# Pairwise dot products on TensorE: one product of four samples on 128 columns, or four products of one sample on 32 columns each

## The reference

```python
e = jnp.stack([tbl_0[ids[:, 0]], ..., tbl_31[ids[:, 31]]], axis=1)   # [2048, 32, 256]
dots = jnp.einsum('bnd,bmd->bnm', e, e)
z = dots[:, iu, ju]                        # i < j: 496 values for each sample
h = jnp.concatenate([z, dense_ctx], axis=1)                          # [2048, 512]
h = jnp.maximum(h @ W_top1 + b_top1, 0.0)                            # 512 -> 512
h = jnp.maximum(h @ W_top2 + b_top2, 0.0)                            # 512 -> 256
y = h @ W_top3                                                       # 256 -> 1
```

## Time and profile before

| | |
|---|---|
| median of 3 runs | 632.87 us (630.38 to 633.89) |
| profiled execution | 631.31 us, of it the span from the first to the last instruction 629.3 us |
| mean granted TensorE clock | 0.986 of full speed |
| busy: TensorE, weight loads | 558.0 us, 548.1 us |
| busy: GpSimd | 440.0 us |
| busy: VectorE, ScalarE | 358.6 us, 283.0 us |
| DMA | 70.29 MB, mean 112 GB/s |

### The profile page before, as it was taken

One profiled execution on the slowest core, in us unless ns is written; L12 is line 12 of the kernel. 1 busy time (PEld: TensorE's weight loads), 2 busy tenths in 40 slices (PEclk: granted clock), 3 DMA queues, 4 the chain that ended last, 5 costly groups with the idle time before them and its releaser, 6 DMA issues.

```text
span 629.3 us, 11634 instructions
## 1 busy us (share of the span) xinstructions
PE 558.0 (89%) x4752; PEld 548.1 (87%) x4752; DVE 358.6 (57%) x772; ACT 283.0 (45%) x497; POOL 440.0 (70%) x462
## 2 busy tenths in 40 slices
PE   0345989998999999999999999999999999998973
PEld 0335989898999999999999999999999999998973
DVE  0163846746476574838486675848385665735330
ACT  0171644543455454545454454546354454545330
POOL 6787777777777777777777777777777777777000
PEclk9999999998999999999999999999999999999987
DMA  8963443344444643446334543446334643355000
GB/s 197 266 186 92 113 119 110 115 88 133 113 117 111 93 138 106 125 100 120 112 117 115 100 132 102 127 95 125 113 115 116 82 147 105 107 94 120 2 1 0
DMA packets 35407, 70.29 MB, mean 112 GB/s; under 512 B 15655, under 2 KB 19751, under 8 KB 34855
## 3 DMA queue, kind: packets, MB, share of 16 engines
q0 software_dynamic: 21888, 59.80, 38.1%
q1 hardware_dynamic: 13466, 9.75, 6.4%
HBM read 69.51 MB, written 0.01 MB: 110 GB/s over the span
## 4 chain that ended last, share of the span: by engine, by line
PE 40%; POOL 39%; issue 13%; DMA 4%; DVE 2%; ACT 1%; DVEq 0%; POOLq 0%
POOL rows L236 39%; PE gram_ps L272 16%; PE sel_ps L326 8%; PE tr_ps L251 7%; PE gram_ps L294 5%; DMA rows<-in_tbl,ids_sb 4%; PE gram_ps L304 3%; DVE dots L383 1%; PE gram_ps L283 1%; DVE onehot L437 1%; PE gram_ps L312 1%; ACT dots L383 0%; DVE dots_t L445 0%; DVE emb_t L373 0%; DMA ids_sb<-in_ids 0%
## 5 line engine op out<-in xcount | busy, mean ns | idle before, releaser
L236 POOL DMA_INDIRECT rows<-in_tbl,ids_sb x456 | 439.3, 963 | 140.2 <-issue 136.5
L272 PE MATMUL gram_ps<-emb_t 128*128 128x124 f32 x2048 | 242.3, 278 | 0.3 <-DVE y_sb L472 0.3
L272 PEld LDWEIGHTS gram_ps<-emb_t 128*128 128x128 f32 x2048 | 237.3, 195 | 0.4 <-issue 0.4
L366 DVE COPY emb_t<-tr_ps 128x512 f32<-128x512 f32 x114 | 129.7, 1138 | 83.3 <-PE tr_ps L251 82.2
L251 PE MATMUL tr_ps<-ident,rows 128*128 128x128 f32 x912 | 127.6, 286 | 47.5 <-DMA rows<-in_tbl,ids_sb 47.5
L366 ACT COPY emb_t<-tr_ps 128x512 f32<-128x512 f32 x114 | 129.7, 1138 | 65.6 <-PE tr_ps L251 64.1
L383 ACT COPY dots<-gram_ps 32x124 f32<-32x124 f32 x256 | 96.1, 375 | 136.3 <-PE gram_ps L272 134.0
L251 PEld LDWEIGHTS tr_ps<-ident,rows 128*128 128x128 f32 x912 | 109.3, 149 | 52.6 <-DMA rows<-in_tbl,ids_sb 33.3
L383 DVE COPY dots<-gram_ps 32x124 f32<-32x124 f32 x256 | 94.5, 369 | 58.5 <-PE gram_ps L272 55.9
L326 PE MATMUL sel_ps<-onehot,sel_high 125*128 125x256 f32 x448 | 110.8, 288 | 6.2 <-DVE emb_t L373 6.2
L326 PE MATMUL sel_ps<-onehot,sel_low 125*128 125x256 f32 x448 | 108.6, 283 | 0.0
(11 more groups left out here) (19 smaller groups left out, 108.4 us busy)
## 6 DMA issues: line engine op xcount, KB each, us to landing
rows<-in_tbl,ids_sb POOLq DMA_INDIRECT x456, 2.8
emb_t<-in_tbl SPq DMA_DIRECT2D x4, 896.0 KB
sel_ids<-in_ids_by_field SPq DMA_DIRECT2D x28, 128.0 KB, 3.4
w_sb<-in_W_top SPq DMA_DIRECT2D x1, 1024.0 KB, 28.9
w_sb<-in_W_top SPq DMA_DIRECT2D x1, 512.0 KB, 30.6
emb_t<-in_tbl SPq DMA_DIRECT2D x4, 104.0 KB
packed<-in_dense_ctx SPq DMA_DIRECT2D x16, 8.0 KB, 1.8
ids_sb<-in_ids SPq DMA_DIRECT2D x1, 240.0 KB, 3.1
```

The costliest lines, as they stand in the source:

```text
L236: pool.indirect_dma_start(out=rows[g % RING][:, j, :], out_offset=None, in_=tables[f], in_offset=bass.IndirectOffsetOnAxis(ap=ids_sb[:, t, ...
L272: last = nc.tensor.matmul(gram_out[k][:, g, :], four.rearrange("p s f -> p (s f)"), four[:, :, 0:firsts], start=(h == 0), stop=(h == D_HAL ...
L366: copy(emb_t[t % PAIR][:, h, :, at[0]:at[-1] + 1].rearrange("p (g s) f -> p f s g", s=QUAD), tr_ps[h][g % 2][:, 0:len(at), :].rearrange("p ...
```

## The change

A product now takes one sample (`TILED = 1`): its stationary operand is that sample's 32 rows, its moving operand the same sample's 31 first fields, and its result goes to partitions 32c to 32c+31 of PSUM, where c is the sample's place in its group. So the 128 columns of the array are used as four column tiles of 32. A group has four products for each half of the values instead of one. Since the four results of a group stand below each other in the same 31 columns, a group takes 31 words of a bank instead of 124; a fill has 8 groups instead of 4, there are 4 fills for a tile instead of 8, and a fill leaves PSUM in one copy of 128x248 instead of four copies of 32x124 for each of two fills. VectorE copies fills 0 and 2, ScalarE fills 1 and 3.

```diff
+TILED = 1
...
-    bank_groups = 4
+    bank_groups = 8
...
-        gram_ps = [psum(f"gram_ps{k}", [P, bank_groups * P]) for k in range(2)]
-        gram_out = [gram_ps[k][:, 0:bank_groups * QUAD * firsts].rearrange("p (g n) -> p g n", g=bank_groups)
+        gram_ps = [psum(f"gram_ps{k}", [P, QUAD * P]) for k in range(2)]
+        gram_out = [gram_ps[k][:, 0:bank_groups * TILED * firsts].rearrange("p (g n) -> p g n", g=bank_groups)
                     for k in range(2)]
...
                 for g in range(bank_groups):
                     s = (fill * bank_groups + g) * QUAD
                     for h in range(D_HALVES):
-                        four = emb_t[u][:, h, s:s + QUAD, :]
-                        last = nc.tensor.matmul(gram_out[k][:, g, :], four.rearrange("p s f -> p (s f)"),
-                                                four[:, :, 0:firsts], start=(h == 0), stop=(h == D_HALVES - 1))
+                        for c in range(0, QUAD, TILED):
+                            own = emb_t[u][:, h, s + c:s + c + TILED, :]
+                            last = nc.tensor.matmul(gram_out[k][c * fields:(c + TILED) * fields, g, :],
+                                                    own.rearrange("p s f -> p (s f)"), own[:, :, 0:firsts],
+                                                    start=(h == 0), stop=(h == D_HALVES - 1))
                 last.then_inc(gram_done[k], 1)
...
-                for k in range(fills_each):
-                    turning(k)
-                    gram(t - 1, 2 * k)
-                    gram(t - 1, 2 * k + 1)
+                for fill in range(fills):
+                    turning(fill)
+                    gram(t - 1, fill)
                 turning(4)
...
-            for s in range(QUAD):
-                own = slice(s * fields, (s + 1) * fields)
-                last = copy(dots[own, :, fill * bank_groups:(fill + 1) * bank_groups].rearrange("p f g -> p g f"),
-                            gram_out[k][own, :, s * firsts:(s + 1) * firsts])
-            last.then_inc(dots_copied[k], 1)
+            copy(dots[:, :, fill * bank_groups:(fill + 1) * bank_groups].rearrange("p f g -> p g f"),
+                 gram_out[k]).then_inc(dots_copied[k], 1)
...
                     emb_copy(dve, 0, copy, t, k)
-                    dots_copy(dve, 0, copy, t - 1, k)
+                    if k % 2 == 0:
+                        dots_copy(dve, 0, copy, t - 1, k // 2)
...
                     emb_copy(act, 1, copy, t, k)
...
-                    dots_copy(act, 1, copy, t - 1, k)
+                    if k % 2 == 1:
+                        dots_copy(act, 1, copy, t - 1, k // 2)
```

More of the change, by code:

```diff
@@ L59, in build @@
     assert width == D_HALVES * P and features == k1 * P and fields == groups == P // QUAD
-    assert k1 == 4 and m1 == 4 and m2 == 2 and tiles % PAIR == 0 and fills_each == 4
+    assert k1 == 4 and m1 == 4 and m2 == 2 and tiles % PAIR == 0 and fills_each == 2 and fills == QUAD
     order = field_order(fields)
@@ L449, in period @@
                 halves = [(job, half) for job in jobs(t) for half in range(2)]
-                for k in range(fills_each):
+                for k in range(fills):
                     emb_copy(dve, 0, copy, t, k)
-                    dots_copy(dve, 0, copy, t - 1, k)
+                    if k % 2 == 0:
+                        dots_copy(dve, 0, copy, t - 1, k // 2)
                     for job, half in halves[k:k + 1]:
```

## The result

| | before | changed |
|---|---|---|
| median of the runs | 631.68 us (630.38 to 633.89) | 641.76 us (636.28 to 645.6) |
| profiled execution, its span | 631.31, 629.3 us | 641.92, 639.9 us |
| mean granted TensorE clock | 0.986 | 0.874 |

The ratio is 1.0145, with a 95% interval from 1.0106 to 1.0184: slower by 1.5%, a small loss but a clear one, where 626.5 us and a gain had been forecast. The time lies inside the range, near the 640 us of its rival 1.

What follows compares the result with a forecast made beforehand. TensorE and GpSimd were taken to bound the kernel together at 35.0 us a tile. With TensorE at 33.5, only the end gains, 3.0 + 2.4 + 0.8 = 6.2 us: 626.5 us forecast, range 619 to 717.

Steps and rivals of the forecast that it cites:

- rival 1: Dots: column tiles don't overlap; 28 ns a pair gives 640 us, 32 ns gives 673; chance 0.20.
- What bounds the kernel before: Steady part: TensorE and GpSimd stand at the bound together, 35.0 us for a tile each.
- The distance s: Dots: time from one load and matmul pair to the next, bounded by 18 and 56 ns, taken as 24.
- the rival worked out by that rule: Dots: loading and streaming don't overlap on column tiles; 56 ns a pair, 49.9 us a tile, 870 us; chance 0.13.
- The last tile: End: the last tile's dots, with nothing beside them, fall from 14.8 us to 12.3 + 0.1, a gain of 2.4.
- the proportional case: Dots: the load shrinks with its columns and loads follow one another, 28 ns a pair.
- The dots of an inner tile: Inner tiles: 12.3 us of dots instead of 14.3, plus 1.0 us for changes of array shape.
- rival 5: Dots: tiles overlap better; 18 ns a pair gives 623.5 us, 10 ns 619.5; chance 0.47 together with the forecast.
- TensorE's sum: Steady part: 34.5 - 14.3 + 12.3 + 1.0 = 33.5 us for a tile, against GpSimd's 35.0.
- Switches: Between dots and transposes: 8 changes of array shape a tile, at most 1.3 us, taken as 1.0.
- Copies: VectorE and ScalarE: two copies of 0.62 us each a tile, 4.7 us less; the 0.5 us one-hot wait goes.
- The clock: TensorE: smaller products might lose the granted clock earlier, which would make the forecast wrong; no size given.

Runs made afterwards that it cites:

- the spread tiny products: The kernel before with 192 extra 1x1 products for each tile, 8 in each of 24 places between the groups of its dots: 882.22 us.

## Why the prediction was wrong, step by step

**What bounds the kernel before** held. TensorE and GpSimd stand at the bound together; GpSimd's last gather ended at 583.4 us in the changed kernel for 580.9, and it was TensorE that fell behind.

**The distance s.** It was bounded from below by 18 ns, and 24 was taken. Inside a burst it is 8 to 10, so the lower end was wrong: 9 ns for an instruction had been read from the earlier trace rows as the limit of the dispatch, but those rows show only that 8 instructions took no longer than that, not that they could not be faster. The Trainium skill's rule in "TensorEngine Tiling (Array Packing)", Tiling Modes, Key Properties, that tiles load and multiply in parallel, agrees with the trace: four pairs of products of one sample take about 40 ns, and one of the old pairs 112. The Trainium skill's rule in "TensorE: Matmul & The Clock Gate", Part 3, The mechanism, against overlap within one row group, doesn't hold here: all four tiles use the same rows, and the rival worked out by that rule had 56 ns for a pair. Rival 1 gave about the right time, but its tiles that don't overlap are refuted by the same 8 to 10 ns; its number was met by luck.

**The last tile** came out as forecast, but not for the reason given. 12.3 us were predicted and 12.3 measured; they are four blocks of instructions, not 512 array steps. Two errors cancelled: an s from the array that was too large, and a supply that had been left out of the sum. The supply's price, 28 ns a pair, is the number that had stood as the proportional case.

**The dots of an inner tile, 12.3 + 1.0 us in the sum for TensorE, are the step that failed**: the sum has no term for time in which TensorE has no instructions or is held up. The prediction named the supply in its rival 5, one packet for every 128 pairs, "some 3 us at s = 24" apart, and left a slower fetch to rival 1. A packet needs 3.6 us when nothing disturbs, and then the inner tile is as forecast: the even phases of 13 to 17 us are around the 16.0 that 12.3 of dots, 1.0 of switches and 2.7 of three quads of transposes make. What was missing altogether is the stores of y at the start of the dots in every odd period. The forecast didn't ask what else uses the DMA engines there. The six odd phases from the fifth on took 19 to 25 us, some 25 us more in all than in the kernel before, while the six even ones had gained 15. The kernel before felt the stores little: it needs a block only every 14 us, and its phases from the fourth on are 17.1 us but for two odd ones of 17.6 and 17.7.

**TensorE's sum** of 33.5 us for a tile was thus too low. From the sixth to the fourteenth period's dots it measured (536.1 - 246.0)/8 = 36.3 us, over GpSimd's 35.0. TensorE lost its slack, and the last dots started at 605.80 instead of 591.23, 14.6 us later, where 3.0 us earlier had been forecast. The rest of the end was as told: last dots 14.76 to 12.33, -2.4; last copy 1.46 to 0.57, -0.9; 0.7 less behind it. 14.6 - 2.4 - 0.9 - 0.7 = 10.6 us, the difference of the spans.

**Switches** were put at 1.0 us for a tile, 0.13 each; the spread tiny products gave 0.13. In the changed kernel the median step from the last transpose of a quad to the first product is 0.20 us, and the one back 0.13, where two transposes follow each other at 0.11 and two products at 0.01: 0.8 us for a tile's eight. **Copies**: 0.62 forecast, 0.588 and 0.604 measured; the wait for one-hot rows is gone from the groups. Neither matters at GpSimd's pace.

**The clock** was named as a danger without a price. The mean is 0.874, and it falls behind the waits: 1.00 from 606 to 608 us, 0.57 in the next two, where the first wait of the last dots ends, then 0.50. Transposes are busy for 142.6 instead of 127.6 us and the select products for 227.6 instead of 219.4, 23 us in all or 1.5 us for a tile. It isn't the cause: without the inner stores it is still 0.89, and the kernel takes 627.5 us, one microsecond from the forecast. That nearness is in part luck too, since the last dots start there at 591.0 us and not the 3.0 us earlier that the forecast had.

## What to carry to other kernels

Count instructions, not only array time, when a product is cut into smaller ones: here TensorE's program came in blocks of 256 instructions, some 3.6 us apart when it used them up faster, and below 14 ns for an instruction the supply sets the pace. Two samples for a product halved the instructions, needed four copies again, and beat the kernel before by 0.9 to 1.5%. Then look at what small DMAs stand where an engine is short of instructions; moving seven stores of 1 KB was worth as much as the whole change had cost. And where a kernel is held by another engine's fixed pace, price an edit only where it stands alone, at the end.

## What the runs showed of the hardware

A store of 256 results of 4 bytes each holds up other queues: an instruction packet of 16 KB behind it took up to 5.1 us (6.6 in another run), for about 1.1 otherwise, or started some 4 us late, and a quad of gathered rows was waited for 3.4 us. It also stopped TensorE inside a packet that was there already, in five of seven odd periods; the way isn't shown. TensorE's instructions come in packets of 256, and the next packet starts about 1.1 us behind the first use of the one before. Four column tiles really work side by side: 8 to 10 ns for a pair of load and multiply, against 25 for tiny pairs in one place and 112 for full ones. Two tiles of 64 columns need 30 ns for a pair, so a sample costs more there by the array, and less by the supply. At a granted clock of 0.50 a pair on four tiles takes 13 ns, while tiny pairs in one place stay at 25.
